# An attention kernel: the product with v in two 64-row tiles of TensorE, two key chunks by 512 queries a slot

## The chip, the cores and the metric

One Trainium2 chip, one of its cores. The metric is the device time of the whole kernel in microseconds (us). Engines are named as the profile names them: PE is TensorE (PEld its weight loads), DVE VectorE, ACT ScalarE, POOL GpSimd, SP the queue that issues the DMAs.

## What is computed

Two attention layers, one behind the other, over 4 images of 128 channels by 32 x 32 positions (1024). Both layers have the same form, with their own weights:

```python
q = jnp.einsum('rc,bcn->brn', Wq, xf) + bq[None, :, None]      # 16 x 1024
k = jnp.einsum('rc,bcn->brn', Wk, xf) + bk[None, :, None]      # 16 x 1024
v = jnp.einsum('oc,bcn->bon', Wv, xf) + bv[None, :, None]      # 128 x 1024
attn = jax.nn.softmax(jnp.einsum('bri,brj->bij', q, k), axis=2)
out = jnp.einsum('bcj,bij->bci', v, attn)
x = gamma * out + x
```

## The kernel before

The work is cut into 8 stages, one for each layer and image (stages 0 to 3 are layer 0, 4 to 7 layer 1; stage s + 4 reads what stage s wrote). A stage s has these items:

- QK: q and k from x, in three fp32r products of high and low parts (x_hi, x_lo made by POOL). DVE adds the bias in two steps, mask and stack, into qk; stack also frees the PSUM bank pair that QK wrote. SP copies qk into the layouts for the energies (qk_swapped, q_shifted, k_twice).
- E 0 to 7: energies of 128 queries by 1024 keys, two matmuls of 64 rows each, which stand on two row tiles of TensorE and write two banks. DVE takes the maximum ("max"), ACT exponentiates and sums ("sum").
- shift: the maxima and the logs of the sums are transposed on PE, split by DVE ("rows") and put into spare rows of q_shifted by a DMA.
- ET 0 to 7: transposed energies, again two matmuls of 64 rows; ACT exponentiates them into attn ("attn"), which is now the normalised attention of 128 keys by 1024 queries.
- V: v for all keys, in fp32, 8 matmuls; DVE adds the bias ("v32"), ACT and DVE split it (v_hi, v_lo).
- PV 0 to 7: attention times v, summed over the 8 slots in out_psum (two banks). Two slots (0 and 7) are native: fp32, which the chip runs as two passes for each matmul. The six others are cut: attn is split into attn_hi (by ACT for slots 2, 4, 6, else POOL) and attn_lo (by POOL), and three fp32r products are added. In the last stage DVE makes both parts of slots 1, 3 and 6 ("cut" in its order).
- finish 0 and 1: DVE multiplies out_psum by gamma and adds x, for a half of 512 queries each.

Every engine runs its items in an order written out by hand: a list for the start (PE_FIRST, DVE_FIRST and so on), then one list that is repeated in each step (PE_STEP, DVE_STEP); an item ("PV", 0, 3) in step s is slot 3 of stage s + 0. So one step of PE holds the rest of PV of one stage, ET of the next, E of the one after, and QK of the third. Semaphores order the engines among each other: an engine waits in its own order, so whatever stands behind a waiting instruction waits too.

PSUM has 8 banks: out_psum takes two, and three pairs form a ring that QK, E, ET, V and shift use in turn, in PE's order. Each use waits until the use three turns before it has been read (wait_for_ring, L243): for QK that is DVE's stack, for E ACT's sum, for ET ACT's attn.

The places that matter here: PE_STEP (L64), DVE_STEP (L92), finish (L522), energies_transposed (L622), times_v (L633). In times_v the first slot of a stage waits for the finish of the half before it (L652), and the lines of a cut slot wait for attn_hi first and attn_lo ahead of the third product (L653).

## Time and profile before

| | us |
|---|---|
| median of 3 runs | 220.22 |
| lowest, highest | 219.42, 221.62 |
| span of the profiled execution, first to last instruction | 219.6 |
| mean granted TensorE clock | 0.977 |
| PE busy | 203.2 (93%) |
| ACT busy | 167.8 (76%) |
| POOL busy | 160.0 (73%) |
| DVE busy | 151.4 (69%) |

Busy time is the sum of an engine's instruction times without overlap. The granted clock is what the throttle leaves TensorE, as a share of full speed. The profile shows a start of some 60 us in which the stages fill up, five like steps of 22.7 us, and an end in which no new stage comes in.

The profile's line of a matmul gives the rows and columns of the array that it uses, as 64*128, and the shape of its moving operand, as 64x512. In a timeline, "x4" means four instructions merged in one line, and the time is that from the first start to the last end. A native matmul shows as two instructions.

### The profile page before, as it was taken

To read this page: it belongs to the slowest core of one execution; us is meant where nothing else is said; L and a number is where in the kernel's file an instruction comes from. 1 tells how busy PE (TensorE), PEld (TensorE's weight loads), DVE (VectorE), ACT (ScalarE), POOL (GpSimd) and SP (SyncE) were. 2 spreads that over 40 slices of the span, in tenths; PEclk is the share of its full clock that TensorE was granted. 3 is DMA by queue.
4 is the path that set the end of the run, shared out by engine and by line. 5 is a ranking of instruction groups with operands and counts; after the bars stand their busy time and mean duration, and the time that the engine had idled before them with its cause. 6 is when DMAs were issued, how large, how long until landed. Compare 5 with 4: busy or idle time off the path is not lost.

```text
span 219.6 us, 2538 instructions
## 1 busy us (share of the span) xinstructions
PE 203.2 (93%) x874; PEld 116.7 (53%) x876; DVE 151.4 (69%) x145; ACT 167.8 (76%) x244; POOL 160.0 (73%) x87
## 2 busy tenths in 40 slices
PE   6766978797999999999999999999999999999994
PEld 1542423245565656565666466646564656565581
DVE  1599599674767777686768676867686749406972
ACT  2221479888999996999699969998799898958500
POOL 1780000069999799979997999799999957982950
PEclk9796799999999999999999999999999999999999
DMA  6807030009309200930075006600480710050202
...
DMA packets 6142, 17.15 MB, mean 78 GB/s; under 512 B 1008, under 2 KB 1392, under 8 KB 6128
## 3 DMA queue, kind: packets, MB, share of 16 engines
...
q14 instruction: 7, 0.06, 0.1%
...
## 4 chain that ended last, share of the span: by engine, by line
PE 80%; DVE 11%; DMA 3%; issue 2%; ACT 2%; SPq 1%; ACTq 0%
PE out_psum L656 47%; PE ring L628 9%; PE ring L605 8%; PE ring L594 6%; PE ring L577 5%; DVE neg_max L494 5%; DMA x_all<-x_in 2%; PE out_psum L666 2%; DVE masked_hi L449 1%; ACT attn L399 1%; DVE shift_masked L502 1%; PE ring L618 1%; DMA q_shifted<-shift_rows 1%; DVE shift_rows L506 1%; DVE qk L454 1%
## 5 line engine op out<-in xcount | busy, mean ns | idle before, releaser
L348 POOL TENSOR_TENSOR attn_lo<-attn,attn_hi 128x1024 fp32r<-128x1024 f32 x45 | 110.2, 2467 | 10.0 <-ACT attn_hi L405 8.1
L494 DVE TENSOR_REDUCE neg_max<-ring 128x1 f32<-128x1024 f32 x64 | 76.2, 1220 | 27.3 <-PE ring L607 27.1
L379 ACT ACTIVATE ring<-ring,neg_max 128x1024 f32<-128x1024 f32 x64 | 69.8, 1090 | 19.1 <-DVE neg_max L494 18.8
L399 ACT ACTIVATE attn<-ring 128x1024 f32<-128x1024 f32 x64 | 62.9, 1022 | 11.1 <-PE ring L630 11.1
L342 POOL TENSOR_SCALAR attn_hi<-attn 128x1024 fp32r<-128x1024 f32 x22 | 24.1, 1094 | 30.2 <-ACT attn L399 30.2
L605 PE MATMUL ring<-qk_swapped,qk 64*128 64x512 f32 x64 | 28.7, 466 | 6.6 <-DVE qk_swapped L454 4.2
L656 PE MATMUL out_psum<-attn_hi,v_hi 128*128 128x512 f32 x96 | 33.8, 433 | 0.0
L656 PE MATMUL out_psum<-attn,v 128*128 128x512 f32 x64 | 31.4, 614 | 0.0
L656 PE MATMUL out_psum<-attn_hi,v_lo 128*128 128x512 f32 x96 | 30.0, 394 | 0.0
L656 PE MATMUL out_psum<-attn_lo,v_hi 128*128 128x512 f32 x96 | 29.9, 393 | 0.0
L607 PE MATMUL ring<-qk,qk_swapped 64*128 64x512 f32 x64 | 28.7, 466 | 0.0
L628 PE MATMUL ring<-q_shifted,k_twice 64*128 64x512 f32 x64 | 25.7, 458 | 0.9 <-DMA q_shifted<-shift_rows 0.9
L630 PE MATMUL ring<-q_shifted,k_twice 64*128 64x512 f32 x64 | 25.7, 458 | 0.0
L605 PEld LDWEIGHTS ring<-qk_swapped,qk 64*128 64x128 f32 x64 | 11.5, 187 | 23.8 <-issue 8.1
L405 ACT CAST attn_hi<-attn 128x1024 fp32r<-128x1024 f32 x23 | 24.0, 1046 | 0.2
L656 PEld LDWEIGHTS out_psum<-attn_hi,v_hi 128*128 128x128 f32 x96 | 15.2, 188 | 12.1 <-issue 10.8
L656 PEld LDWEIGHTS out_psum<-attn_lo,v_hi 128*128 128x128 f32 x96 | 18.1, 188 | 4.2
L656 PEld LDWEIGHTS out_psum<-attn_hi,v_lo 128*128 128x128 f32 x96 | 18.1, 188 | 4.1
L666 PE MATMUL out_psum<-zeros 128*128 128x512 bf16 x52 | 18.0, 442 | 1.7 <-POOL zeros L317 1.3
L628 PEld LDWEIGHTS ring<-q_shifted,k_twice 64*128 64x128 f32 x64 | 10.2, 184 | 14.5 <-issue 9.6
L656 PEld LDWEIGHTS out_psum<-attn,v 128*128 128x128 f32 x64 | 11.1, 189 | 12.6 <-issue 12.2
L594 PEld LDWEIGHTS ring<-late,x_all 128*128 128x128 f32 x128 | 15.4, 192 | 4.5 <-issue 4.3
...
## 6 DMA issues: line engine op xcount, KB each, us to landing
...
q_shifted<-shift_rows SPq DMA_DIRECT2D x16, 8.0 KB
```

Source lines behind the costliest of these rows:

```text
L342: nc.gpsimd.tensor_scalar(attn_hi[:, j - NATIVE], attn[:, j], 1.0, 0.0, ALU.mult, ALU.add).then_inc(hi_made["gpsimd"], 1)
L348: nc.gpsimd.tensor_tensor(attn_lo[:, j - NATIVE], attn[:, j], attn_hi[:, j - NATIVE].bitcast(fp32), ALU.subtract).then_inc(lo_made["gpsimd ...
L379: nc.scalar.activation(e[:], e[:], ACT.Exp, bias=neg_max[s % 2][:, i:i + 1], accum_out=row_sum[s % 2][:, i:i + 1]).then_inc(sum_made, 1)
L399: nc.scalar.activation(attn[:, j], ring_tile("ET", s, k)[:], ACT.Exp).then_inc(attn_made, 1)
L405: nc.scalar.copy(attn_hi[:, j - NATIVE], attn[:, j]).then_inc(hi_made["scalar"], 1)
L494: nc.vector.tensor_reduce(neg_max[s % 2][:, i:i + 1], ring_tile("E", s, i)[:], axis=AX.X, op=ALU.max, negate=True).then_inc(max_made, 1)
L594: last = nc.tensor.matmul(to[:, j * C:(j + 1) * C], x_all[:, s, j * P:(j + 1) * P], late[:, l, :], start=True, stop=True)
L605: nc.tensor.matmul(to[:, 0:HALF], qk[p][0:64, rows], qk_swapped[p][0:64, 0:HALF], start=True, stop=True)
L607: nc.tensor.matmul(to[:, HALF:N], qk_swapped[p][64:128, rows], qk[p][64:128, HALF:N], start=True, stop=True).then_inc(e_mm, 1)
L628: nc.tensor.matmul(to[:, 0:HALF], k_twice[p][0:64, rows], q_shifted[p][0:64, 0:HALF], start=True, stop=True)
L630: nc.tensor.matmul(to[:, HALF:N], k_twice[p][64:128, rows], q_shifted[p][64:128, HALF:N], start=True, stop=True).then_inc(et_mm, 1)
L656: last = nc.tensor.matmul(out_psum[:, part], v, a[:, part], start=(k == 0 and n == 0), stop=(k == TILES - 1 and n == len(passes) - 1))
```

## The change

PV now works in 64-row matmuls as well. Each product of 128 keys is done as two matmuls, keys 0 to 63 of the chunk on the upper row tile into bank 0 of out_psum, keys 64 to 127 on the lower into bank 1; both hold the same 512 queries, and the two banks are added at the end. A slot is therefore two key chunks (a pair of PAIRS) by one half of the queries: slots 0 to 3 are half 0, slots 4 to 7 half 1. ET writes its two banks to match: chunk one and chunk two, same 512 queries. Native are slots 0 and 7 as before.

finish of a half is two additions, the second reading what the first wrote. out_psum holds one half at a time, so slot 4 of a stage waits for finish of half 0 and slot 0 of the next stage for finish of half 1. In the orders, finish of half 0 moves in DVE_STEP from the end to behind the maximum of E 3, and in PE_STEP PV 3 stands ahead of QK. In the cuts of attn by POOL, ACT and DVE and in the bias of stage 0 only the indices change (slot k instead of chunk ORDER[k]).

```diff
-ORDER = [0, 2, 3, 4, 5, 6, 7, 1]
+
+PAIRS = [0, 1, 2, 3, 1, 2, 3, 0]
+SLOTS = TILES // 2
+
+
+def half_of(k):
+    return slice(k // SLOTS * HALF, (k // SLOTS + 1) * HALF)
+
+
+def native(k):
+    return PAIRS[k] == 0
...
 PE_STEP = [
-    ("QK", 3, 0), ("PV", 0, 3), ("ET", 1, 0), ("ET", 1, 1), ("PV", 0, 4), ("ET", 1, 2), ("ET", 1, 3),
+    ("PV", 0, 3), ("QK", 3, 0), ("ET", 1, 0), ("ET", 1, 1), ("PV", 0, 4), ("ET", 1, 2), ("ET", 1, 3),
...
 DVE_STEP = [
     ("v32", 1, 0), ("cut", 0, 3), ("rows", 1, 0), ("max", 2, 0), ("cut", 0, 6), ("max", 2, 1),
-    ("max", 2, 2), ("max", 2, 3), ("mask", 3, 0), ("cut", 1, 1), ("stack", 3, 0), ("max", 2, 4),
-    ("v_lo", 1, 0), ("max", 2, 5), ("max", 2, 6), ("max", 2, 7), ("finish", 0, 0), ("finish", 0, 1),
+    ("max", 2, 2), ("max", 2, 3), ("finish", 0, 0), ("mask", 3, 0), ("cut", 1, 1), ("stack", 3, 0), ("max", 2, 4),
+    ("v_lo", 1, 0), ("max", 2, 5), ("max", 2, 6), ("max", 2, 7), ("finish", 0, 1),
...
-        attn = sb("attn", [P, TILES, N])
-        attn_hi = sb("attn_hi", [P, CUT, N], fp32r)
-        attn_lo = sb("attn_lo", [P, CUT, N], fp32r)
+
+        attn = sb("attn", [P, TILES, 2, HALF])
+        attn_hi = sb("attn_hi", [P, CUT, 2, HALF], fp32r)
+        attn_lo = sb("attn_lo", [P, CUT, 2, HALF], fp32r)
...
-        pv_half_mm, pv_mm, x_made, stored = sem("pv_half_mm"), sem("pv_mm"), sem("x_made"), sem("stored")
+        x_half_made, pv_mm, x_made, stored = sem("x_half_made"), sem("pv_mm"), sem("x_made"), sem("stored")
...
         def hi_on(s, k):
 
-            if ORDER[k] < NATIVE:
+            if native(k):
                 return None
             if s == STAGES - 1 and k in LAST_BY_VECTOR:
                 return "vector"
...
             def attention(s, k):
-                j = ORDER[k]
                 act.wait_ge(et_mm, TILES * s + k + 1)
 
-                if j < NATIVE:
+                if native(k):
                     at_least(act, pv_mm, TILES * (s - 1) + k + 1)
                 elif s > 0:
                     wait_for_lo(act, s - 1, k)
-                nc.scalar.activation(attn[:, j], ring_tile("ET", s, k)[:], ACT.Exp).then_inc(attn_made, 1)
+                nc.scalar.activation(attn[:, k], ring_tile("ET", s, k)[:].rearrange("p (a n) -> p a n", a=2),
+                                     ACT.Exp).then_inc(attn_made, 1)
...
             def finish(s, h):
 
-                dve.wait_ge(pv_half_mm if h == 0 else pv_mm, s + 1 if h == 0 else TILES * (s + 1))
+                dve.wait_ge(pv_mm, TILES * s + SLOTS * (h + 1))
                 gamma, part = columns[:, GAMMA + layer(s):GAMMA + layer(s) + 1], slice(h * HALF, (h + 1) * HALF)
-                nc.vector.scalar_tensor_tensor(out=x_all[:, s + B if s < B else s, part], in0=out_psum[:, part], scalar=gamma,
-                                               in1=x_all[:, s, part], op0=ALU.mult,
-                                               op1=ALU.add).then_inc(x_made, 1)
+                to = x_all[:, s + B if s < B else s, part]
+                nc.vector.scalar_tensor_tensor(out=to, in0=out_psum[:, 0:HALF], scalar=gamma, in1=x_all[:, s, part],
+                                               op0=ALU.mult, op1=ALU.add).then_inc(x_half_made, 1)
+                dve.wait_ge(x_half_made, 2 * s + h + 1)
+                nc.vector.scalar_tensor_tensor(out=to, in0=out_psum[:, HALF:N], scalar=gamma, in1=to,
+                                               op0=ALU.mult, op1=ALU.add).then_inc(x_made, 1)
...
             def energies_transposed(s, k):
-                p, j, to = s % 2, ORDER[k], ring_tile("ET", s, k)
-                rows = slice(j * P, (j + 1) * P)
+                p, to, part = s % 2, ring_tile("ET", s, k), half_of(k)
+                first, second = (slice((2 * PAIRS[k] + n) * P, (2 * PAIRS[k] + n + 1) * P) for n in range(2))
                 if k == 0:
                     pe.wait_ge(shift_placed, 32 * (s + 1))
                 wait_for_ring(pe, "ET", s, k)
-                nc.tensor.matmul(to[:, 0:HALF], k_twice[p][0:64, rows], q_shifted[p][0:64, 0:HALF],
+                nc.tensor.matmul(to[:, 0:HALF], k_twice[p][0:64, first], q_shifted[p][0:64, part],
                                  start=True, stop=True)
-                nc.tensor.matmul(to[:, HALF:N], k_twice[p][64:128, rows],
-                                 q_shifted[p][64:128, HALF:N], start=True, stop=True).then_inc(et_mm, 1)
+                nc.tensor.matmul(to[:, HALF:N], k_twice[p][64:128, second],
+                                 q_shifted[p][64:128, part], start=True, stop=True).then_inc(et_mm, 1)
 
             def times_v(s, k):
-                p, j = s % 2, ORDER[k]
+                p = s % 2
                 if k == 0:
                     pe.wait_ge(v_made, s + 1)
-                if j < NATIVE:
+                if k % SLOTS == 0:
+                    at_least(pe, x_made, 2 * s + k // SLOTS)
+                if native(k):
                     pe.wait_ge(attn_made, TILES * s + k + 1)
-                    passes = ((v32[p][:, j], attn[:, j]),)
+                    passes = [(v32[p][:, n], attn[:, k, n]) for n in range(2)]
                 else:
                     wait_for_hi(pe, s, k)
-                    c = j - NATIVE
-                    passes = ((v_hi[p][:, c], attn_hi[:, c]), (v_lo[p][:, c], attn_hi[:, c]),
-                              (v_hi[p][:, c], attn_lo[:, c]))
-
-                work = [(n, h) for n in range(len(passes)) for h in range(2)]
-                if k == TILES - 1:
-                    work.sort(key=lambda nh: nh[1])
-                for n, h in work:
-                    part = slice(h * HALF, (h + 1) * HALF)
-                    if k == 0 and n == 0:
-                        at_least(pe, x_made, 2 * (s - 1) + h + 1)
-                    if n == 2 and h == 0:
+                    c = 2 * PAIRS[k] - NATIVE
+                    passes = [(v[p][:, c + n], attn_hi[:, k - 1, n]) for v in (v_hi, v_lo) for n in range(2)]
+                    passes += [(v_hi[p][:, c + n], attn_lo[:, k - 1, n]) for n in range(2)]
+                for n, (v, a) in enumerate(passes):
+                    if n == 4:
                         wait_for_lo(pe, s, k)
-                    v, a = passes[n]
-                    last = nc.tensor.matmul(out_psum[:, part], v, a[:, part], start=(k == 0 and n == 0),
-                                            stop=(k == TILES - 1 and n == len(passes) - 1))
-                    if k == TILES - 1 and (n, h) == (len(passes) - 1, 0):
-                        last.then_inc(pv_half_mm, 1)
+                    start = k % SLOTS == 0 and n == 0
+                    stop = k % SLOTS == SLOTS - 1 and n == len(passes) - 1
+                    nc.tensor.matmul(out_psum[:, 0:HALF], v[0:64], a[0:64], start=start, stop=stop)
+                    last = nc.tensor.matmul(out_psum[:, HALF:N], v[64:128], a[64:128], start=start, stop=stop)
                 last.then_inc(pv_mm, 1)
```

PE's order in a steady step, of before, from E 3 (the pair L605 and L607) through QK (L577) and PV 3 (L656) to ET 0 (L628, L630):

```order
L605 MATMUL ring<-qk_swapped,qk 128x512
L607 MATMUL ring<-qk,qk_swapped 128x512
L577 MATMUL ring<-x_hi,wqk_hi 128x512 x2
L577 MATMUL ring<-x_hi,wqk_lo 128x512 x2
L577 MATMUL ring<-x_lo,wqk_hi 128x512 x2
L656 MATMUL out_psum<-attn_hi,v_hi 128x512 x2
L656 MATMUL out_psum<-attn_hi,v_lo 128x512 x2
L656 MATMUL out_psum<-attn_lo,v_hi 128x512 x2
L628 MATMUL ring<-q_shifted,k_twice 128x512
L630 MATMUL ring<-q_shifted,k_twice 128x512
```

The same place in the changed kernel, from the last four matmuls of PV 3 (L661 upper row tile, L662 lower) on; QK is L586, ET is L637 and L639:

```order
L661 MATMUL out_psum<-attn_lo,v_hi 128x512
L662 MATMUL out_psum<-attn_lo,v_hi 128x512
L661 MATMUL out_psum<-attn_lo,v_hi 128x512
L662 MATMUL out_psum<-attn_lo,v_hi 128x512
L586 MATMUL ring<-x_hi,wqk_hi 128x512 x2
L586 MATMUL ring<-x_hi,wqk_lo 128x512 x2
L586 MATMUL ring<-x_lo,wqk_hi 128x512 x2
L637 MATMUL ring<-q_shifted,k_twice 128x512
L639 MATMUL ring<-q_shifted,k_twice 128x512
```

PV 3 has moved ahead of QK, and its six matmuls of 128 rows have become twelve of 64 rows, alternating between the row tiles.

DVE's order in the last stage, of before; L513 and L518 are the two parts of a cut, L526 a finish:

```order
L513 CAST attn_hi<-attn 128x1024
L518 TENSOR_TENSOR attn_lo<-attn,attn_hi 128x1024
L513 CAST attn_hi<-attn 128x1024
L518 TENSOR_TENSOR attn_lo<-attn,attn_hi 128x1024
L526 SCALAR_TENSOR_TENSOR x_all<-out_psum,weights,x_all 128x512 x2
```

And in the changed kernel, with what each waits for; L520 and L524 are the cut, L533 and L536 the two additions of a finish:

```order
L520 CAST attn_hi<-attn 128x1024 [waits pv_mm,attn_made]
L524 TENSOR_TENSOR attn_lo<-attn,attn_hi 128x1024 [waits hi_made_vector]
L520 CAST attn_hi<-attn 128x1024 [waits pv_mm,attn_made]
L524 TENSOR_TENSOR attn_lo<-attn,attn_hi 128x1024 [waits hi_made_vector]
L533 SCALAR_TENSOR_TENSOR x_all<-out_psum,weights,x_all 128x512 [waits pv_mm]
L536 SCALAR_TENSOR_TENSOR x_all<-out_psum,weights,x_all 128x512 [waits x_half_made]
L533 SCALAR_TENSOR_TENSOR x_all<-out_psum,weights,x_all 128x512 [waits pv_mm]
L536 SCALAR_TENSOR_TENSOR x_all<-out_psum,weights,x_all 128x512 [waits x_half_made]
```

The two finishes have become four additions. The place of the cuts ahead of finish of half 0 is as before; what is new is that PE's slot 4 waits for that finish.

## Rows read from the trace of the kernel before

**Rows 1.** Busy time by stretch: length, engines' busy us (instructions), clock, DMA share, GB/s.
```profile
119.75:142.50 22.75, 22.67 (x105) 13.59 (x103) 16.45 (x17) 20.59 (x31) 21.21 (x11) 1.00 0.32 71
```

**Rows 2.** Chain that ended last: start us, us on it, engine and line.
```profile
105.27 0.43 PE ring L605
105.70 1.59 PE ring L577 x6
107.29 1.39 PE out_psum L656 x6
...
138.84 0.23 PE ring L605
139.07 1.92 PE out_psum L656 x4
140.99 1.78 PE ring L594 x16
...
216.39 0.75 DVE x_all L526
```

**Rows 3.** Timeline of a steady step: start us, us, engine, line, operation [idle before].
```profile
127.94 0.50 PE L605 MATMUL ring<-qk_swapped,qk 64*128 64x512 f32 x1
127.94 0.50 PE L607 MATMUL ring<-qk,qk_swapped 64*128 64x512 f32 x1
...
129.40 0.62 PE L577 MATMUL ring<-x_lo,wqk_hi 128*128 128x512 f32 x2
...
130.07 1.34 DVE L463 TENSOR_SCALAR masked_hi<-ring,weights 128x1024 fp32r<-128x1024 f32 x1 [0.36 <-PE ring L577]
...
131.44 1.28 DVE L471 SCALAR_TENSOR_TENSOR qk<-ring,weights,masked_hi 128x1024 fp32r<-128x1024 f32 x1
...
133.60 0.50 PE L628 MATMUL ring<-q_shifted,k_twice 64*128 64x512 f32 x1
...
134.14 1.94 ACT L399 ACTIVATE attn<-ring 128x1024 f32<-128x1024 f32 x2 [0.31 <-PE ring L630]
...
141.16 1.40 DVE L526 SCALAR_TENSOR_TENSOR x_all<-out_psum,weights,x_all 128x512 f32<-128x512 f32 x2
...
148.12 1.09 ACT L379 ACTIVATE ring<-ring,neg_max 128x1024 f32<-128x1024 f32 x1
```

**Rows 4.** Timeline of the end, from E 3 of stage 7 on.
```profile
173.34 0.50 PE L605 MATMUL ring<-qk_swapped,qk 64*128 64x512 f32 x1
...
185.13 2.02 PE L594 MATMUL ring<-late,x_all 128*128 128x128 f32 x16
...
195.60 0.73 PE L656 MATMUL out_psum<-attn_hi,v_hi 128*128 128x512 f32 x2
...
198.19 1.23 DVE L518 TENSOR_TENSOR attn_lo<-attn,attn_hi 128x1024 fp32r<-128x1024 f32 x1
...
203.78 1.98 PE L656 MATMUL out_psum<-attn,v 128*128 128x512 f32 x4
...
209.03 0.62 PE L656 MATMUL out_psum<-attn_hi,v_hi 128*128 128x512 f32 x2
209.19 2.71 POOL L348 TENSOR_TENSOR attn_lo<-attn,attn_hi 128x1024 fp32r<-128x1024 f32 x1
...
209.69 3.30 DVE L518 TENSOR_TENSOR attn_lo<-attn,attn_hi 128x1024 fp32r<-128x1024 f32 x1
...
215.53 1.61 DVE L526 SCALAR_TENSOR_TENSOR x_all<-out_psum,weights,x_all 128x512 f32<-128x512 f32 x2 [2.54 <-PE out_psum L656]
```

**Rows 5.** TensorE's idle time in the start, and the granted clock behind it.
```profile
18.66 0.79 PE L605 MATMUL ring<-qk_swapped,qk 64*128 64x512 f32 x1 [4.16 <-DVE qk_swapped L454]
...
18.00:20.00 2.00, 1.34 (x4) 0.42 (x4) 2.00 (x4) 0.00 (x0) 0.00 (x0) 0.59 0.96 227
20.00:22.00 2.00, 2.00 (x6) 0.85 (x6) 1.68 (x2) 1.09 (x2) 0.00 (x0) 0.50 1.04 248
...
24.00:26.00 2.00, 1.75 (x6) 0.48 (x6) 1.28 (x2) 0.00 (x0) 0.00 (x0) 0.70 0.00 0
```

More of the change, by code:

```diff
@@ L208, in lo_on @@
         def lo_on(s, k):
-            if ORDER[k] < NATIVE:
+            if native(k):
                 return None
@@ L338, in attn_hi_of @@
             def attn_hi_of(s, k):
-                j = ORDER[k]
                 pool.wait_ge(attn_made, TILES * s + k + 1)
                 at_least(pool, pv_mm, TILES * (s - 1) + k + 1)
-                nc.gpsimd.tensor_scalar(attn_hi[:, j - NATIVE], attn[:, j], 1.0, 0.0, ALU.mult,
+                nc.gpsimd.tensor_scalar(attn_hi[:, k - 1], attn[:, k], 1.0, 0.0, ALU.mult,
                                         ALU.add).then_inc(hi_made["gpsimd"], 1)
             def attn_lo_of(s, k):
-                j = ORDER[k]
                 wait_for_hi(pool, s, k)
-                nc.gpsimd.tensor_tensor(attn_lo[:, j - NATIVE], attn[:, j],
-                                        attn_hi[:, j - NATIVE].bitcast(fp32),
+                nc.gpsimd.tensor_tensor(attn_lo[:, k - 1], attn[:, k],
+                                        attn_hi[:, k - 1].bitcast(fp32),
                                         ALU.subtract).then_inc(lo_made["gpsimd"], 1)
@@ L370, in add_bias0 @@
                         act.wait_ge(qk0_mm, 2 * n + h + 1)
-                        nc.scalar.activation(attn[:, n, part], ring_tile(use, 0, 0)[:, part], ACT.Identity,
+                        nc.scalar.activation(attn[:, n, h], ring_tile(use, 0, 0)[:, part], ACT.Identity,
                                              bias=weights[:, QK_SETS * P + bias:QK_SETS * P + bias + 1]
@@ L448, in _ @@
                         dve.wait_ge(stacked0_made, h + 1)
-                    nc.vector.tensor_scalar(masked_hi[:, part], attn[:, n, part], columns[:, mask:mask + 1], 0.0,
+                    nc.vector.tensor_scalar(masked_hi[:, part], attn[:, n, h], columns[:, mask:mask + 1], 0.0,
                                             ALU.mult, ALU.add).then_inc(masked0_made, 1)
@@ L453, in _ @@
                     dve.wait_ge(masked0_made, 2 * n + h + 1)
-                    nc.vector.tensor_tensor(to[:, part], attn[:, n, part], masked_hi[:, part].bitcast(fp32),
+                    nc.vector.tensor_tensor(to[:, part], attn[:, n, h], masked_hi[:, part].bitcast(fp32),
                                             ALU.subtract).then_inc(stacked0_made, 1)
@@ L509, in attn_hi_of @@
             def attn_hi_of(s, k):
-                j = ORDER[k]
                 dve.wait_ge(attn_made, TILES * s + k + 1)
                 at_least(dve, pv_mm, TILES * (s - 1) + k + 1)
-                nc.vector.tensor_copy(attn_hi[:, j - NATIVE], attn[:, j]).then_inc(hi_made["vector"], 1)
+                nc.vector.tensor_copy(attn_hi[:, k - 1], attn[:, k]).then_inc(hi_made["vector"], 1)
             def attn_lo_of(s, k):
-                j = ORDER[k]
                 wait_for_hi(dve, s, k)
-                nc.vector.tensor_tensor(attn_lo[:, j - NATIVE], attn[:, j],
-                                        attn_hi[:, j - NATIVE].bitcast(fp32),
+                nc.vector.tensor_tensor(attn_lo[:, k - 1], attn[:, k],
+                                        attn_hi[:, k - 1].bitcast(fp32),
                                         ALU.subtract).then_inc(lo_made["vector"], 1)
             def finish(s, h):
-                dve.wait_ge(pv_half_mm if h == 0 else pv_mm, s + 1 if h == 0 else TILES * (s + 1))
+                dve.wait_ge(pv_mm, TILES * s + SLOTS * (h + 1))
                 gamma, part = columns[:, GAMMA + layer(s):GAMMA + layer(s) + 1], slice(h * HALF, (h + 1) * HALF)
-                nc.vector.scalar_tensor_tensor(out=x_all[:, s + B if s < B else s, part], in0=out_psum[:, part], scalar=gamma,
-                                               in1=x_all[:, s, part], op0=ALU.mult,
-                                               op1=ALU.add).then_inc(x_made, 1)
+                to = x_all[:, s + B if s < B else s, part]
[4 more added lines that the diff above has]
+                                               op0=ALU.mult, op1=ALU.add).then_inc(x_made, 1)
             for what, s, i in in_order(DVE_FIRST, DVE_STEP):
@@ L633, in times_v @@
             def times_v(s, k):
-                p, j = s % 2, ORDER[k]
+                p = s % 2
                 if k == 0:
                     pe.wait_ge(v_made, s + 1)
-                if j < NATIVE:
+                if k % SLOTS == 0:
+                    at_least(pe, x_made, 2 * s + k // SLOTS)
+                if native(k):
                     pe.wait_ge(attn_made, TILES * s + k + 1)
-                    passes = ((v32[p][:, j], attn[:, j]),)
+                    passes = [(v32[p][:, n], attn[:, k, n]) for n in range(2)]
```

4 lines of the change are left out of this document (1 added, 3 removed).

## The prediction

> **What bounds the kernel now.** I read the busy time by stage first. In a full step of the steady part TensorE is busy 22.67 of 22.75 us, ScalarE 20.59, GpSimd 21.21, VectorE 16.45 [rows 1]. So TensorE sets the step, and ScalarE and GpSimd stand only 2.1 and 1.5 us under it: what TensorE can lose per step is capped by them. Next I read the chain that ended last, which runs through TensorE nearly all the way, for what a matmul costs by its neighbours [rows 2]. A pair of 64-row matmuls (both start at 127.94 in [rows 3]) takes 0.23 us when it follows another pair, and 0.43 when it stands alone among 128-row work. Six 128-row matmuls take 1.39 us behind other 128-row work and 1.59 where they stand next to a pair. So a passage between the two row shapes costs about 0.2 us each way over both sides together: (0.43 - 0.23) + (1.59 - 1.39) = 0.4 us for going into 128 rows and back. One unsplit pass of an fp32 (native) slot takes (1.92 - 0.2) / 4 = 0.43 us. The third view is the timeline of one step, for who waits behind whom [rows 3], and the fourth the timeline of the end, where stage 7 has no other work beside it [rows 4].
>
> **What the change takes off TensorE.** A steady step has eight 128-row groups: QK+PV 3, PV 4, PV 5, PV 6, PV 7+V, PV 0+shift, PV 1, PV 2. With PV in 64-row pairs three are left (QK, V, shift): five fewer, 5 x 0.4 = 2.0 us. A cut slot is now 6 pairs of 0.23 instead of 6 matmuls of 0.23: 1.39 us either way. That price is a pair's behind a pair [rows 2]; the trace has no more than three in a row, so it could be higher, not lower.
>
> **What it adds.**
> (a) Native slots, two per step. Each product is two passes on the same row tile, and the program order is both passes of the upper tile, then both of the lower. Starts follow program order in the timeline, so the lower tile's first pass starts with the upper tile's second, one pass late. The lower tile then ends after 5 passes instead of 4: 2.14 us for 1.71. No row shows fp32 in 64 rows, so the bounds are 1.71 (full overlap) and 8 x 0.43 = 3.42 (none). I take 2.14: + 0.43 twice, 0.86 us per step.
> The page "TensorE: Matmul & The Clock Gate" of the Trainium skill, Part 3 (Packing small matmuls), gives matmuls packed into different tiles the span of one and some 4 ns. By that a native slot would cost 1.71 and the sum below would be that of rival 2, 219.9 us instead of 223.2. The same part says that matmuls keep program order in start and end, by which the lag stands. No row of this case decides between them.
> (b) A wait behind QK. Count from the start of pair E 3 (127.94 in [rows 3]). Before: QK at 0.43, its end 2.1, mask to 3.5, stack to 4.78 (131.44 + 1.28), ET 2 takes QK's ring bank at 5.66; 0.9 us to spare. After: PV 3 stands ahead, QK runs 1.72 to 3.37, mask 3.42 to 4.76, stack to 6.07. TensorE reaches ET 2 at 1.72 + 1.6 + 0.23 x 2 + 0.1 + 1.39 = 5.28 and waits till 6.12: + 0.84. Behind ET 2 stand ET 3, E 4 and PV 5, and ScalarE, which finds no attention tile until 6.6 (6.2 before).
> (c) finish of half 0. VectorE adds twice: 2 x 0.70 us (the pair of additions at 215.53 has one wait in it; the pair at 141.16 takes 1.40 [rows 3]). PV 4 waits for it. In a steady step PV 3 ends at 1.8, finish runs 1.83 to 3.3, and PV 4 comes at 3.9 because QK and two ET pairs lie between: nothing. Its cover is QK. finish of half 1 is as long as both finishes before, and V (1.78 us) lies between PV 7 and the next PV 0: nothing.
> Step: 22.74 - 2.0 + 0.86 + 0.84 = 22.4 us. ScalarE, from ET 2 at 6.12, needs 0.5 for the pair and then the 15 us it ran without a pause from 134.14 to 149.2 [rows 3] till the bank of E 3 is free: a bound of about 21.95; it does not decide. GpSimd's 21.2 does not either. Gain 0.3 us in each of the five steps with QK (they end at E 3 at 173.34): 1.5 us. Ahead of them PV 1 and PV 2 of stage 0 stand between pairs: 0.7 us. Together 2.2 us.
>
> **The end, counted from E 3 at 173.34 [rows 4].** From here there is no QK, and from stage 6 no V.
> - PV 4 of stage 5 waits for finish until 3.33, since no QK covers it. The passages saved repay that; V starts at 11.8 (185.13) on both sides, after by ScalarE's sum that frees its bank.
> - Stage 6: PV 3 ends at 21.4, as before. finish takes till 23.05 with two ET pairs as cover, so PV 4 starts at 23.1 (22.26 before). PV 7 ends at 30.1; before stage 7's PV 0 stands finish of half 1 (1.45 us) with two ET pairs as cover: 31.8 (30.4 before). PV 3 of stage 7 ends at 38.3 (37.05, since its six matmuls from 209.03 take 1.36).
> - Stage 7 is the large one. VectorE has two cuts there (attention tiles 3 and 6) **ahead of** finish of half 0, and PV 4 now waits for that finish. Before, nothing waited for it. The second cut ends at 212.99 = 39.65, since it comes through only 1.1 us after GpSimd's 2.71 us cut at 209.19 ends (3.30 us, where the same cut took 1.23 at 198.19 with GpSimd idle). GpSimd's row of cuts starts when ScalarE has made its copies, which hardly moves: 39.6. finish to 41.05, and PV 4 starts at 41.1: TensorE stands still for 2.8 us. This is the last stage's own order: in the other stages VectorE has no cuts.
> - Then 3 x 1.39 + 2.14 = 6.3 us of PV, 0.2, two additions one behind the other 1.45 (one of 0.75 at 216.39 before [rows 2]), and 2.46 us from the last addition to the end as now (219.6 - 217.14): 51.5 us. Before: 46.26. **+ 5.2 us.**
>
> **Sum.** 219.6 - 2.2 + 5.2 = 222.6 us of span. The median of the runs is 220.22, 0.6 above the profiled span, so 223.2 us: 1.4% slower. About 1% is what a measurement here can tell from no change.
>
> **Rivals.**
> 1. *The clock falls in the stop.* At the start TensorE idles 4.16 us before 18.66 and the granted clock is 0.59 and 0.50 of full in the two stretches behind (0.50 is the 1.2 GHz level of 2.4), and 0.70 between 24 and 26 [rows 5]. The new stop is 2.8 us (shorter: against), but with two short ones ahead of it (for). 6.3 us of PV at half speed for 3 to 6.3 us costs 1.5 to 3.1 us more: 225.5 us.
> 2. *Native pairs overlap fully.* Then a slot is 1.71, TensorE's step 21.6, ScalarE's 21.95 decides: 0.8 x 5 + 0.7 = 4.7 us gained, and the end costs 4.4 (0.43 less for each of the two or three native slots on its path, partly waited away): 219.3 + 0.6 = 219.9, no change. For it: all 64-row pairs in the trace start together. Against: those are one pass each.
> 3. *Faster.* As 2, and the second cut of stage 7 comes through before GpSimd's third instead of after it: 2.7 us earlier, with the stop gone but for some tenths. 219.9 - 2.7 = 217.2, and any further gain in the steps, whose cap is GpSimd's 21.2, is on top: about 216.8. It decides from the point where VectorE's cut starts before 209.1. Against it: the cut at 209.69 started after.
> 4. *No overlap of fp32 between the row tiles.* 16 slots x (3.42 - 2.14) = 20 us: 243 us. Nothing speaks for it but that no row shows the form.
>
> **Chances.** Forecast 0.38, clock 0.22, full overlap 0.18, faster 0.10, no overlap 0.06, something else 0.06. The steps' 0.3 us is the difference of larger terms and may be 0.1 to 0.8, so the forecast's own range is 221 to 224.5, and a third of it lies within 1%. That gives faster 0.12, same 0.30, slower 0.58. The range 218.3 to 227.5 leaves out no overlap, most of the faster case and the clock's far end.
>
> **What would show it.** Right: passages of 0.2 us only around QK, V and shift; cut slots of 1.4 us; in native slots the lower tile's first pass 0.43 behind the upper's; ET 2 waiting for VectorE's stack about 0.8 us in each of five steps; a step of 22.4; PV 4 of stage 7 waiting about 3 us for an addition that stands behind a cut on VectorE; 2.2 us gained at the last E 3. Wrong: pairs of PV at more than 0.25 us; both tiles of a native slot starting together; a step under 22; a clock under 1.00 at the end; a cut that ends before 209.

## The result, and the profile after

The changed kernel takes 223.23 us (median of 4 runs, 221.69 to 224.22); before, timed beside it, takes 220.37 us. The ratio is 1.0121, 95% interval [1.0076, 1.0166]: slower by 1.2%. The total stands on the forecast, but not for the reasons given: the gain in the steps and the loss at the end were each forecast too small, by some 3 and 1.5 us, and the two errors cancel. The profiled run took 222.52 us with a span of 220.7 us.

First the page of the kernel after: of its part 1 the busy time and share of the span, of its part 2 (the span in 40 slices, each digit a share in tenths) the rows of TensorE and of its granted clock.

```profile
PE 191.9 (87%) x1226; PEld 121.3 (55%) x1228; DVE 164.6 (75%) x161; ACT 165.8 (75%) x244; POOL 159.6 (72%) x87
PE   7717789897999998999899989998998999788392
PEclk9975799999999999999999999999999999999978
```

TensorE is busy 11 us less than before (191.9 for 203.2) and the span is 1.1 us longer: the work saved went into waiting. VectorE has 13 us more, the second additions. Near the end TensorE falls to 3 tenths of a slice, and in the last two slices the granted clock, which had been full since the start, falls too.

The busy time of one steady step (columns: busy time and instructions of PE, PEld, DVE, ACT and POOL, then granted clock, DMA share and GB/s), for the 22.75 us row in [rows 1]:

```profile
124.09:145.95 21.86, 21.13 (x150) 14.00 (x148) 18.41 (x19) 20.23 (x31) 21.15 (x12) 1.00 0.33 74
```

TensorE is busy 21.13 of 21.86 us. The idle rest is one wait. It is in the timeline of the same step, of VectorE and TensorE (start, duration, engine, line; the brackets give the idle time ahead and what ended it), for [rows 3]:

```profile
125.64 0.73 PE L586 MATMUL ring<-x_hi,wqk_hi 128*128 128x512 f32 x2
125.76 0.75 DVE L533 SCALAR_TENSOR_TENSOR x_all<-out_psum,weights,x_all 128x512 f32<-128x512 f32 x1 [0.16 <-PE out_psum L662]
...
127.35 1.34 DVE L471 TENSOR_SCALAR masked_hi<-ring,weights 128x1024 fp32r<-128x1024 f32 x1
127.81 0.39 PE L661 MATMUL out_psum<-attn_hi,v_hi 64*128 64x512 f32 x1
128.73 1.28 DVE L479 SCALAR_TENSOR_TENSOR qk<-ring,weights,masked_hi 128x1024 fp32r<-128x1024 f32 x1
130.07 0.49 PE L637 MATMUL ring<-q_shifted,k_twice 64*128 64x512 f32 x1 [0.72 <-DVE qk L479]
```

PV 3 ends, the two additions of finish 0 run at 125.76 and 126.55 under QK, PV 4 at 127.81 waits for nothing, and ET 2 waits 0.72 us for the stack. 21.13 + 0.72 is the step.

The ends of matmuls are modelled in the trace, so a short stop can be hidden in busy time; the starts show it. A pair that follows a pair without a wait starts 0.23 us after it. Twice in a step it takes longer, because the pair's weight load waits for ScalarE to empty a ring bank (in brackets):

```profile
132.60 0.18 PEld L614 LDWEIGHTS ring<-qk_swapped,qk 64*128 64x128 f32 x1 [0.39 <-ACT attn L407]
134.61 0.18 PEld L614 LDWEIGHTS ring<-qk_swapped,qk 64*128 64x128 f32 x1 [0.33 <-ACT attn L407]
```

E 5 starts 0.35 us behind ET 4 and PV 6 0.34 behind E 5; E 7 starts 0.28 behind E 6 and PV 7 0.34 behind E 7. Together that is 0.39 us a step over four times 0.23, none of it shown as idle. By the same measure the stop at ET 2 costs 0.98 us, not 0.72: ET 2 starts 1.11 us behind the last pair of PV 4, and ET 3 0.34 behind ET 2.

A native slot in the same timeline, the form that no row of before showed:

```profile
134.95 0.59 PE L661 MATMUL out_psum<-attn,v 64*128 64x512 f32 x1
134.95 0.59 PE L662 MATMUL out_psum<-attn,v 64*128 64x512 f32 x1
```

The two row tiles start together in every pass, to 0.01 us (the three left out stand at 135.38, 135.80 and 136.23): 4 x 0.43 = 1.71 us, with no lag.

The end, for [rows 4]. The timeline shows first VectorE and GpSimd, then what TensorE waited for:

```profile
199.04 2.69 DVE L520 CAST attn_hi<-attn 128x1024 fp32r<-128x1024 f32 x1
...
202.72 3.23 POOL L357 TENSOR_TENSOR attn_lo<-attn,attn_hi 128x1024 fp32r<-128x1024 f32 x1
203.63 2.87 DVE L520 CAST attn_hi<-attn 128x1024 fp32r<-128x1024 f32 x1
206.53 1.23 DVE L524 TENSOR_TENSOR attn_lo<-attn,attn_hi 128x1024 fp32r<-128x1024 f32 x1
207.67 0.75 DVE L533 SCALAR_TENSOR_TENSOR x_all<-out_psum,weights,x_all 128x512 f32<-128x512 f32 x1
...
190.70 0.50 PE L661 MATMUL out_psum<-attn_hi,v_hi 64*128 64x512 f32 x1 [1.17 <-DVE x_all L536]
199.22 0.66 PE L661 MATMUL out_psum<-attn,v 64*128 64x512 f32 x1 [1.22 <-issue]
209.26 0.79 PE L661 MATMUL out_psum<-attn_hi,v_hi 64*128 64x512 f32 x1 [3.70 <-DVE x_all L536]
```

TensorE is through with PV 3 of stage 7 at 205.56 (209.26 - 3.70); the two additions that PV 4 waits for start only at 207.67, because the cut of slot 6 is ahead of them on VectorE. The stops of 1.17 us (PV 4 of stage 6) and 1.22 us (PV 0 of stage 7) stand behind finish too, with two ET pairs as cover. The busy time of the same end by stretch, with the granted clock as the third number from the right:

```profile
206.00:208.00 2.00, 0.00 (x0) 0.00 (x0) 1.97 (x3) 0.00 (x0) 0.00 (x0) 1.00 0.00 0
208.00:210.00 2.00, 0.74 (x4) 0.65 (x6) 1.17 (x2) 0.00 (x0) 0.00 (x0) 0.69 0.00 0
210.00:212.00 2.00, 2.00 (x14) 1.51 (x12) 0.00 (x0) 0.00 (x0) 0.00 (x0) 0.50 0.38 139
212.00:214.00 2.00, 2.00 (x20) 1.65 (x18) 0.00 (x0) 0.00 (x0) 0.00 (x0) 0.96 0.00 0
```

After the stop the clock is 0.50 of full, 1.2 GHz of 2.4, for a while. The last four slots take 7.5 us (209.26 to the addition at 216.76).

### The profile page after: what moved, and what is told of

Its sections match the earlier page's. It is cut to its first block, busy times and chain, and to the rows that moved or that the text cites. A ratio compares the mean times of both kernels' runs of the same rounds, so it can differ in the third digit from the quotient of the medians.

```text
span 220.7 us, 3266 instructions
## 1 busy us (share of the span) xinstructions
PE 191.9 (87%) x1226; PEld 121.3 (55%) x1228; DVE 164.6 (75%) x161; ACT 165.8 (75%) x244; POOL 159.6 (72%) x87
## 3 DMA queue, kind: packets, MB, share of 16 engines
HBM read 2.69 MB, written 2.10 MB: 22 GB/s over the span
## 4 chain that ended last, share of the span: by engine, by line
PE 66%; DVE 23%; issue 4%; DMA 3%; ACT 2%; SPq 1%; ACTq 0%
PE out_psum L661 31%; PE ring L614 7%; PE ring L637 7%; PE ring L603 6%; DVE neg_max L502 6%; PE ring L586 5%; PE out_psum L662 5%; DVE masked_hi L471 4%; DVE qk L479 3%; DVE attn_hi L520 3%; PE out_psum L669 2%; DMA x_all<-x_in 2%; DVE masked_hi L457 2%; DVE x_all L533 2%; DVE x_all L536 1%
## 5 line engine op out<-in xcount | busy, mean ns | idle before, releaser
L502 DVE TENSOR_REDUCE neg_max<-ring 128x1 f32<-128x1024 f32 x64 | 75.4, 1218 | 14.3 <-PE ring L616 13.9
L407 ACT ACTIVATE attn<-ring 128x1024 f32<-128x1024 f32 x64 | 62.9, 1024 | 13.7 <-PE ring L639 13.7
L661 PE MATMUL out_psum<-attn_hi,v_hi 64*128 64x512 f32 x96 | 30.6, 399 | 5.7 <-DVE x_all L536 5.7
L661 PE MATMUL out_psum<-attn,v 64*128 64x512 f32 x64 | 30.2, 591 | 1.2 <-issue 1.2
L662 PE MATMUL out_psum<-attn_hi,v_hi 64*128 64x512 f32 x96 | 30.6, 399 | 0.0
L662 PE MATMUL out_psum<-attn,v 64*128 64x512 f32 x64 | 30.2, 592 | 0.0
L661 PE MATMUL out_psum<-attn_hi,v_lo 64*128 64x512 f32 x96 | 30.1, 394 | 0.0
L662 PE MATMUL out_psum<-attn_hi,v_lo 64*128 64x512 f32 x96 | 30.1, 394 | 0.0
L662 PE MATMUL out_psum<-attn_lo,v_hi 64*128 64x512 f32 x96 | 30.0, 392 | 0.0
L661 PE MATMUL out_psum<-attn_lo,v_hi 64*128 64x512 f32 x96 | 30.0, 392 | 0.0
L637 PE MATMUL ring<-q_shifted,k_twice 64*128 64x512 f32 x64 | 26.0, 459 | 4.4 <-DVE qk L479 3.4
L639 PE MATMUL ring<-q_shifted,k_twice 64*128 64x512 f32 x64 | 26.0, 459 | 0.0
L614 PEld LDWEIGHTS ring<-qk_swapped,qk 64*128 64x128 f32 x64 | 11.9, 186 | 23.9 <-DVE qk_swapped L462 6.5
L533 DVE SCALAR_TENSOR_TENSOR x_all<-out_psum,weights,x_all 128x512 f32<-128x512 f32 x16 | 11.9, 747 | 15.3 <-PE out_psum L662 15.2
L661 PEld LDWEIGHTS out_psum<-attn_hi,v_hi 64*128 64x128 f32 x96 | 18.0, 190 | 9.5 <-DVE x_all L536 6.9
L661 PEld LDWEIGHTS out_psum<-attn_lo,v_hi 64*128 64x128 f32 x96 | 18.0, 187 | 3.2
```

Of the source, the lines that this page charges most:

```text
L407: nc.scalar.activation(attn[:, k], ring_tile("ET", s, k)[:].rearrange("p (a n) -> p a n", a=2), ACT.Exp).then_inc(attn_made, 1)
L502: nc.vector.tensor_reduce(neg_max[s % 2][:, i:i + 1], ring_tile("E", s, i)[:], axis=AX.X, op=ALU.max, negate=True).then_inc(max_made, 1)
L614: nc.tensor.matmul(to[:, 0:HALF], qk[p][0:64, rows], qk_swapped[p][0:64, 0:HALF], start=True, stop=True)
L637: nc.tensor.matmul(to[:, 0:HALF], k_twice[p][0:64, first], q_shifted[p][0:64, part], start=True, stop=True)
L639: nc.tensor.matmul(to[:, HALF:N], k_twice[p][64:128, second], q_shifted[p][64:128, part], start=True, stop=True).then_inc(et_mm, 1)
L661: nc.tensor.matmul(out_psum[:, 0:HALF], v[0:64], a[0:64], start=start, stop=stop)
```

## The experiments

Two questions: what sets the step of 21.86 us and where the passages' 2.0 us went (a passage is the change from 64-row pairs to 128-row matmuls or back), and what the end is made of.

**Passages alone.** PV goes back to 128-row matmuls, and everything else of the change stays: order of the slots, two additions, all waits. Each product of a chunk goes to one bank, in turn.

```
-start = k % SLOTS == 0 and n == 0
-stop = k % SLOTS == SLOTS - 1 and n == len(passes) - 1
-nc.tensor.matmul(out_psum[:, 0:HALF], v[0:64], a[0:64], start=start, stop=stop)
-last = nc.tensor.matmul(out_psum[:, HALF:N], v[64:128], a[64:128], start=start, stop=stop)
+start = k % SLOTS == 0 and n < 2
+stop = k % SLOTS == SLOTS - 1 and n >= len(passes) - 2
+bank = slice(n % 2 * HALF, (n % 2 + 1) * HALF)
+last = nc.tensor.matmul(out_psum[:, bank], v, a, start=start, stop=stop)
```

> The changed kernel with PV's products as 128-row matmuls again, each chunk's whole product into one of the two banks in turn; slots, orders, waits and the two additions as in the changed kernel. Theory (the gain of a step is the passages between 64 and 128 rows): five more groups of 128 rows in a step, 2.0 us more work on TensorE of which the wait behind QK covers up to 0.7, so a step of 22.7 to 23.2 instead of 21.85, and 228 to 230 us in all. Rival (the gain of a step comes from the order alone): step 21.9, 223 us.

Measured: 233.36 us (4 runs), ratio to before 1.0591 [1.0557, 1.0625]. Two steps of it, from VectorE's mask to the next (same columns as above), and its ET 2:

```profile
108.83:132.85 24.02, 22.91 (x104) 13.64 (x105) 19.68 (x20) 20.51 (x30) 20.29 (x12) 1.00 0.30 67
132.85:156.19 23.34, 22.69 (x104) 13.54 (x105) 17.87 (x19) 20.59 (x30) 21.66 (x12) 1.00 0.31 69
```
```profile
135.56 0.49 PE L637 MATMUL ring<-q_shifted,k_twice 64*128 64x512 f32 x1 [0.57 <-DVE qk L479]
```

The steps alternate; their mean is 23.68 us, above the 22.7 to 23.2 expected. What differs between the two kinds is v_lo on VectorE, here in the first step, then in the second, and V on TensorE in the first:

```profile
113.68 3.14 DVE L497 TENSOR_TENSOR v_lo<-v,v_hi 128x768 fp32r<-128x768 f32 x1
137.70 1.06 DVE L497 TENSOR_TENSOR v_lo<-v,v_hi 128x768 fp32r<-128x768 f32 x1
...
119.34 0.91 PE L603 MATMUL ring<-late,x_all 128*128 128x128 f32 x6 [0.45 <-ACT ring L388]
```

At 113.68 v_lo starts just behind a subtraction of GpSimd (113.62) and takes 3.14 us, at 137.70 ahead of one (138.04) and takes 1.06. The maxima behind it come later, ScalarE's sums behind them, and V waits 0.45 us.

Against after (21.86) the mean step is 1.82 us longer, and 1.67 of it is TensorE's busy time (22.80 for 21.13). That is less than five times 0.4, but not because a passage is cheaper: the changed kernel has the two hidden stops for ScalarE (0.39 us) in its 21.13, which this one, with passages in their place, has not. The price itself is in the starts. E 2, PV 2 and the start of E 3, in before with two passages and in after with none:

```profile
125.92 0.50 PE L605 MATMUL ring<-qk_swapped,qk 64*128 64x512 f32 x1
...
144.17 0.39 PE L616 MATMUL ring<-qk,qk_swapped 64*128 64x512 f32 x1
145.79 0.41 PE L616 MATMUL ring<-qk,qk_swapped 64*128 64x512 f32 x1
```

In before it is 2.02 us (125.92 to 127.94, [rows 3]), in after 1.62: 0.40 for the group. So the five groups are 2.0 us, as said. Against before (22.74) the step with 128 rows is 0.9 longer with TensorE's busy time the same within 0.15: the price of the new order and its waits, of which 0.57 is ET 2's and 0.45, in every other step, V's. The 64-row form is worth some 10 us of the kernel (233.36 - 223.23), these waits included; what the new order and the end cost is more.

**The order on TensorE.** QK ahead of PV 3 again, as before the change, and on VectorE mask and stack ahead of finish 0. It takes the wait off ET 2.

```
-("PV", 0, 3), ("QK", 3, 0), ("ET", 1, 0),
+("QK", 3, 0), ("PV", 0, 3), ("ET", 1, 0),
-("max", 2, 3), ("finish", 0, 0), ("mask", 3, 0), ("cut", 1, 1), ("stack", 3, 0), ("max", 2, 4),
+("max", 2, 3), ("mask", 3, 0), ("cut", 1, 1), ("stack", 3, 0), ("finish", 0, 0), ("max", 2, 4),
```

> The changed kernel with QK ahead of PV 3 again, and on VectorE mask and stack ahead of finish of half 0. Theory (QK is the cover of finish, as in the prediction): PV 4 waits until finish ends 6.2 us behind E 3 instead of starting at 3.9, ET 2 starts at 7.6 instead of 5.95, the step grows by about 1.7 us in each of five steps: 231 us. Rival (the wait of ET 2 behind stack is the dearer one): ET 2 waits for nothing, the step shrinks by up to 0.7: 220 us.

Measured: 242.69 us (4 runs), ratio 1.0981 [1.0917, 1.1045]. Its timeline, and its busy time by stretch:

```profile
139.61 0.50 PE L661 MATMUL out_psum<-attn_hi,v_hi 64*128 64x512 f32 x1 [2.18 <-DVE x_all L536]
142.63 1.95 ACT L407 ACTIVATE attn<-ring 128x1024 f32<-128x1024 f32 x2 [3.45 <-PE ring L639]
```
```profile
140.00:142.00 2.00, 2.00 (x14) 1.54 (x12) 0.00 (x0) 0.00 (x0) 2.00 (x2) 0.53 0.96 246
142.00:144.00 2.00, 2.00 (x14) 1.65 (x12) 0.52 (x1) 1.37 (x2) 1.92 (x2) 0.62 1.00 209
```

PV 4 now waits 2.18 us for the additions, as the order says. What I had not counted is what can follow: here the granted clock is 0.53 and 0.62 in the two stretches behind the stop, PV 4's six pairs take 2.35 us (139.61 to 141.96) instead of 1.39, and ScalarE waits 3.45 us for ET 2. It does not follow each time. The five stops of this kind are 2.12 to 2.18 us long; behind three of them the clock falls (those that end at 65.19, 114.68 and 139.61), behind two it stays full (90.68 and 165.01). A step with such a stop and a full clock, then a stop at the end of the run:

```profile
90.68 0.49 PE L661 MATMUL out_psum<-attn_hi,v_hi 64*128 64x512 f32 x1 [2.15 <-DVE x_all L536]
```
```profile
86.51:110.52 24.01, 21.16 (x148) 14.06 (x149) 18.33 (x18) 20.21 (x31) 20.28 (x12) 1.00 0.30 67
```
```profile
209.70 0.79 PE L661 MATMUL out_psum<-attn_hi,v_hi 64*128 64x512 f32 x1 [5.73 <-DVE x_all L536]
```

With a full clock the step is 24.01 us, 2.15 over after's 21.86: the stop and no more. The three with a lower clock are 24.9 to 25.5. Another 4.6 us come from stage 6, whose PV 4 waits 5.73 us where after has 1.17: in this order finish 0 of stage 6 stands behind VectorE's cut of slot 1 of stage 7 as well. So the swap of QK and PV 3 in the change is what keeps finish 0 hidden, and its 0.72 us at ET 2 is the small one of two prices.

**What sets 21.86: ScalarE, VectorE's stack or GpSimd.** Three kernels that each take about 0.5 us or more from one engine in stages where it would show, and leave out a part of the computation: one of ScalarE's copies to a sixteenth, the stack to half its columns, two of GpSimd's subtractions to half.

```
+n = 32 if s in (1, 2, 3, 4) and k == 4 else HALF
+nc.scalar.copy(attn_hi[:, k - 1, :, 0:n], attn[:, k, :, 0:n])
```
```
+n = HALF if s >= 3 else N
+nc.vector.scalar_tensor_tensor(out=qk[s % 2][:, 0:n], in0=ring_tile("QK", s, 0)[:, 0:n], ...
```
```
+n = HALF // 2 if s in (1, 2, 3, 4) and k in (3, 4) else HALF
+nc.gpsimd.tensor_tensor(attn_lo[:, k - 1, :, 0:n], attn[:, k, :, 0:n], ...
```

> The changed kernel with ScalarE's copy of attention tile 4 cut to 64 of 1024 elements in stages 1 to 4 (part of attn_hi is left out). It takes 0.9 us off ScalarE in four steps. Theory A (ScalarE sets the step of 21.86): the step falls to about 21.0 to 21.2. Theory B (TensorE's own order with its wait behind stack sets it): 21.7 to 21.86.

> The changed kernel with VectorE's stack over half the columns in the steps from stage 3's QK on (the other half of qk is left out): 0.6 us less between QK and ET 2. Theory B (the wait of ET 2 is on the chain of the step): ET 2 waits 0.1 instead of 0.7 us and the step falls from 21.86 to 21.2 to 21.3. Theory A (ScalarE sets the step by its work alone): the step stays at 21.7 to 21.86.

> The changed kernel with GpSimd's low parts of attention tiles 3 and 4 over half the elements in stages 1 to 4 (the other half is left out): some 2.4 us less on GpSimd in four steps. If GpSimd, with 21.15 of 21.86 us busy, sets the step, it falls by up to 0.7; by theory A and B alike it stays at 21.86.

Measured, one run each: 222.93, 221.57 and 223.25 us. What counts is the step in the trace, in this order, from mask to mask:

```profile
104.73:126.59 21.86, 21.04 (x148) 13.95 (x149) 18.30 (x18) 19.64 (x30) 21.22 (x11) 1.00 0.33 74
```
```profile
104.81:126.15 21.34, 21.14 (x148) 13.98 (x149) 17.73 (x18) 20.24 (x30) 21.01 (x12) 1.00 0.34 76
```
```profile
104.79:127.00 22.21, 21.30 (x148) 14.01 (x149) 18.83 (x19) 20.39 (x30) 18.48 (x12) 1.00 0.33 73
```

ScalarE's 0.6 us less changes nothing (21.86). The copy stands behind the exponentials for which E 5 and E 7 wait, though, so this run says nothing of those 0.39 us, which are there in all three. The stack's 0.53 us less (0.75 for 1.28 at 127.53) gives 0.52, with ET 2 waiting 0.18: TensorE's 21.14 and that wait. So the step is TensorE's own work, the wait for the stack and, inside the busy time, the two short stops for ScalarE. GpSimd's 2.7 us less makes this step 0.35 us *longer*, and the next one 0.4; the one ahead of them, with the same cut, stays at 21.88. VectorE's v_lo shows why. In the changed kernel, then with less on GpSimd:

```profile
110.35 1.71 DVE L497 TENSOR_TENSOR v_lo<-v,v_hi 128x768 fp32r<-128x768 f32 x1
111.34 2.96 POOL L357 TENSOR_TENSOR attn_lo<-attn,attn_hi 128x1024 fp32r<-128x1024 f32 x1
```
```profile
108.74 2.40 POOL L358 TENSOR_TENSOR attn_lo<-attn,attn_hi 128x1024 fp32r<-128x1024 f32 x1
109.66 2.29 DVE L498 TENSOR_TENSOR v_lo<-v,v_hi 128x768 fp32r<-128x768 f32 x1
```

GpSimd's subtraction has moved over v_lo, which takes 2.29 us instead of 1.71; the maximum behind it comes later, ScalarE waits for it, and TensorE for ScalarE (0.20 us at V). A shift in time on one engine made another slower, by the path that makes the 128-row steps alternate.

**The end, cut behind finish.** VectorE does the cut of slot 6 of the last stage behind finish 0 instead of ahead of it.

```
+late_cut = ("cut", STAGES - 1, 6)
+dve_order.remove(late_cut)
+dve_order.insert(dve_order.index(("finish", STAGES - 1, 0)) + 1, late_cut)
```

> The changed kernel with one item moved on VectorE: in the last stage the cut of slot 6 stands behind finish of half 0. Theory (the order on VectorE makes the stop): PV 4 of stage 7 starts about 2.1 us earlier, the stop shrinks from 3.7 to about 1.6 us, the clock stays at 1.00 there, and the four last slots take 5.9 us instead of 7.3: together 3.5 us less, near 219.7 us. Rival (the contention of VectorE and GpSimd is what is late, whatever the order): the cut of slot 6 is late for PV 6 instead, and 1 us or less is gained.

Measured: 219.57 us (9 runs) beside 220.49 for before (18 runs), ratio 0.9945 [0.9916, 0.9974]; 3.7 us under the changed kernel. Its timeline and the clock:

```profile
207.82 0.68 DVE L520 CAST attn_hi<-attn 128x1024 fp32r<-128x1024 f32 x1
207.96 0.49 PE L665 MATMUL out_psum<-attn_hi,v_hi 64*128 64x512 f32 x1 [1.63 <-DVE x_all L536]
```
```profile
209.00:215.00 6.00, 5.07 (x38) 3.18 (x34) 1.61 (x3) 0.00 (x0) 0.00 (x0) 1.00 0.09 32
```

The stop is 1.63 us, two additions and nothing else, the first part of the cut takes 0.68 us with GpSimd idle instead of 2.87, and the clock stays full. In the traces, from E 3 of stage 7 to the end, it is 49.6 us where after has 53.1.

**The clock apart from the stop.** Twelve small matmuls of zeros into a free bank fill the stop ahead of PV 4 of stage 7; the cut stays ahead of finish.

```
+if (s, k) == (STAGES - 1, SLOTS):
+    pe.wait_ge(attn_made, TILES * STAGES)
+    for _n in range(12):
+        nc.tensor.matmul(ring[0][:, 0:HALF], zeros[:, 0:P], zeros[:], start=True, stop=True)
```

> The changed kernel with 12 matmuls on zeros (bf16, 512 columns, into a free ring bank) in the stop before PV 4 of stage 7. Theory (the clock falls because TensorE stands still): clock 1.00 through the end, PV 4 starts as late as now (the stop is VectorE's), the last four slots take 5.9 us instead of 7.3: 1.4 us less, near 221.8 us. Rival (the clock's fall is not worth anything or not made by the stop): no change, 223.2 us.

Measured: 221.03 us (10 runs), ratio to before 1.003 [1.001, 1.0049]; 2.2 us under the changed kernel. PV 4 starts where it did, 41.6 us behind E 3 (208.92 - 167.31; after: 209.26 - 167.66), and the clock behind it is full (of the twelve matmuls 11 have a record):

```profile
205.36 2.54 PE L649 MATMUL ring<-zeros 128*128 128x512 bf16 x11 [0.16 <-issue]
208.92 0.50 PE L665 MATMUL out_psum<-attn_hi,v_hi 64*128 64x512 f32 x1 [1.02 <-DVE x_all L536]
```
```profile
209.00:212.00 3.00, 3.00 (x27) 2.47 (x28) 0.00 (x0) 0.00 (x0) 0.00 (x0) 1.00 0.25 88
```

From PV 4 to the first addition it is 6.1 us (208.92 to 215.06) where after has 7.5: the clock was worth 1.4 us in the traces, 2.2 by the medians. So of what moving the cut gives (3.4 us in the traces, 3.7 by the medians), 1.4 to 2.2 is the clock and the rest the stop.

**A better end.** The cut of slot 6 stands behind finish 0 as in the experiment above, and on TensorE ET 2 and ET 3 of stage 7 go ahead of PV 4 of stage 6, and ET 7 of stage 7 ahead of its PV 0, so that the stops behind finish have cover.

> The kernel of e1 (cut of slot 6 behind finish of half 0 in the last stage) with three ET of stage 7 moved ahead on TensorE: ET 2 and ET 3 ahead of stage 6's PV 4, ET 7 ahead of stage 7's PV 0, so that they fill the two stops behind finish. Theory: 0.4 to 0.7 us less than e1, near 219.0 us, 0.6 to 0.9% under the kernel before. Rival (the end is set by the cuts on GpSimd and VectorE): no more than e1's 219.6.

Measured: 218.41 us (6 runs) beside 220.34 for before (11 runs), ratio 0.9902 [0.9869, 0.9934]. It is faster than both kernels: 1.0% under before, 2.2% under the changed one. The steps are as in the changed kernel (21.86). From E 3 of stage 7 to the end the trace has 48.9 us, 0.7 less than with the cut alone, as expected. Of the stop of 1.17 us ahead of PV 4 of stage 6, 0.65 is left as a wait of an ET for ScalarE's bank. These stops ahead of PV 0 and PV 4 of stage 7 stay:

```profile
199.19 0.67 PE L674 MATMUL out_psum<-attn,v 64*128 64x512 f32 x1 [1.00 <-issue]
206.91 0.50 PE L674 MATMUL out_psum<-attn_hi,v_hi 64*128 64x512 f32 x1 [1.63 <-DVE x_all L545]
```

**Filling the wait at ET 2.** On top of that kernel, PV 5 goes ahead of ET 2 in each step.

```
-("ET", 1, 1), ("PV", 0, 4), ("ET", 1, 2), ("ET", 1, 3), ("E", 2, 4), ("PV", 0, 5), ("ET", 1, 4),
+("ET", 1, 1), ("PV", 0, 4), ("PV", 0, 5), ("ET", 1, 2), ("ET", 1, 3), ("E", 2, 4), ("ET", 1, 4),
```

> The kernel before this one (218.41 us, step 21.86) with PV 5 moved ahead of ET 2 in every step of TensorE. The wait of 0.72 us at ET 2 for VectorE's stack is then filled: ET 2 would start at 0.51 us later than now (1.39 + 0.23 behind PV 4's end at 128.97 against 130.07) with no wait ahead of it. Theory B (TensorE's own order with that wait sets the step of 21.86): the step falls by 0.72 to about 21.15, less whatever ScalarE takes back. Theory A (ScalarE's chain from ET 2 to the free bank stands right behind): ScalarE, which already waits 0.89 us for ET 2, waits 0.5 us longer, has only 21.86 - 20.23 - 0.71 - 0.89 = 0.03 us left over, and the wait comes back at TensorE as one for ScalarE's sum; the step then goes up by about 0.5 to 22.4. Since ScalarE's instructions fill the step but for these two waits, I expect the second: about 218.4 + 5 x 0.5 = 220.9 us (by theory B 214.8).

Measured: 222.77 us (4 runs), ratio to before 1.0119 [1.0083, 1.0156], 1.9 us above what was expected. A step from mask to mask, and the waits as they stand in the step behind it:

```profile
107.92:130.16 22.24, 21.15 (x148) 14.11 (x150) 17.96 (x19) 20.24 (x30) 21.28 (x12) 1.00 0.33 73
```
```profile
134.84 0.50 PE L650 MATMUL ring<-q_shifted,k_twice 64*128 64x512 f32 x1 [0.65 <-ACT attn L416]
135.75 0.50 PE L627 MATMUL ring<-qk_swapped,qk 64*128 64x512 f32 x1 [0.41 <-ACT attn L416]
```

The step is 0.38 us longer. The wait for the stack is gone, and 0.65 + 0.41 = 1.06 us of waits for ScalarE, at ET 4 and E 5, stand in its place, 0.34 more than the 0.72. PV 5 had been the cover between E 4 and ET 4: without it ET 3, E 4 and ET 4 follow at once, three uses of a ring of three that ScalarE empties at 1 us each. So ScalarE stands right behind the stack, and making ET 2 later costs. Not all five steps are alike: from E 3 to E 3 the first takes 23.6 us, the others 22.2 to 22.5. In the first, v_lo again lies beside a subtraction of GpSimd (3.14 us), and V waits 1.03 us for ScalarE's sum. In all, the steps lose 3.4 us and the end 1.0, the 4.4 us against 218.41.

## Why the prediction came out as it did

- **Passages.** Right, in kind and size: 0.40 us a group in the starts, and 1.67 us of busy time for the five in the experiment with 128 rows, in which after's two hidden stops are missing. Cut slots are six pairs of 0.23, 1.39 us, as said. Between before and after TensorE's busy time falls by 1.54 only (22.67 in [rows 1] to 21.13): 2.0 for the five groups and 0.2 at PV 0, which now goes over into shift at half the price, less 0.39 for the stops at E 5 and E 7 and the 0.26 of ET 2's stop that counts as busy.
- **Native slots, term (a). Wrong.** + 0.86 us per step was 0.00. The inference was that the single passes follow program order, so the lower tile's first pass would come one pass late. The rows show all four passes in pairs. The rule of the Trainium skill, page "TensorE: Matmul & The Clock Gate", Part 3, which gives packed matmuls the span of one and some 4 ns, was the better guide, and I had given it 0.18. The trace of after agrees with it: 0.00 to 0.01 us between the two starts.
- **ET 2 behind QK, mask and stack, term (b).** Right: 0.72 for 0.84 as idle time (0.98 by the starts), and taking 0.53 us off the stack took 0.52 off the step.
- **finish 0 hidden by QK, term (c).** Right in the steady step; taking its cover away cost 2.18 us and the clock behind it.
- **The step.** 22.4 was 21.86: 0.86 less for term (a), 0.12 less for the stack, and 0.46 more because TensorE's busy time, term (a) aside, fell by 1.54 and not by 2.0. The term that was left out is ScalarE's: the prediction had it bound the step from outside (21.95), while it makes two short stops inside TensorE's order, where the passages had been. That 21.86 is near what rival 2 said (21.95) is luck in part: there ScalarE alone decides, and here the stack's stop is the larger one. The steps and the start gave 4.95 us at the last E 3; predicted 2.2, in rival 2 4.7. (173.34 to 167.66 is 5.68, of which 0.73 was there from the first E on: 17.93 for 18.66 in [rows 5]. Both kernels run the same up to there, and x arrives earlier in this run, VectorE's second cast of it at 6.24 for 6.89, so I leave it out as no work of the change.) Of the 4.95, 4.2 is the five steps and 0.7 PV 1 and PV 2 of stage 0, as said.
- **The end.** + 6.8 us (53.0 = 220.7 - 167.66, for 46.26) where 5.2 was said. The mechanism was right: PV 4 of stage 5 at 3.4 us after E 3, V at 11.9 and PV 4 of stage 6 at 23.0 stand within 0.1 us of what was said; PV 4 of stage 7 waits for an addition behind a cut that ends 40.1 us after E 3 (39.6 said), and putting the cut behind it gave 3.7 us. Two sizes were off. The stop was 3.70, not 2.8: TensorE was 0.4 us sooner there, without the native lag, and the additions 0.5 us later. And **rival 1 happened as well**: 0.50 of the clock behind the stop, worth 1.4 us on the last four slots (7.5 us; 6.1 with the stop filled). I had priced it at 1.5 to 3.1 and given it as a case apart, while it went together with the full overlap of rival 2.
- **From span to time.** I added 0.6 us, before's median less its profiled span. But in each run with both numbers the time is 1.8 us above the span (after: 222.52 and 220.7, 221.69 and 219.9). So the profiled run of before was one of about 221.4 us, at the upper end of its range, 0.73 of it by its later first E, and the median run has a span near 218.6.

Put together: the traces give the change itself + 6.8 - 4.95 = + 1.8 us where I had + 5.2 - 2.2 = + 3.0, since 2.75 us of gain and 1.5 us of loss were missed. The medians are 2.9 us apart. The 1.1 us between 1.8 and 2.9 is in neither trace: before's profiled span without its late start (218.9) is 0.3 above that of its median run, and after's (220.7) 0.7 below its own (223.23 - 1.8 = 221.4). After's four runs spread over 2.5 us, and their mean granted clocks (0.965, 0.976, 0.968 and 0.968 for spans of 220.7, 219.9, 222.1 and 222.4) do not order them; only the first has a trace here, so this part stays open. So 223.2 came close by luck, by errors that cancel, and the likeliest case as told was not what happened.
